# Perceiver block on one core: the order of the prelude's steps (first tokens' norm, transposes and queries ahead of the keys' weights and the first context)

## The reference, cut to what matters

```python
x = x + cross_attention(layernorm(x), ctx, ctx, mask)   # 16 heads; ctx is 32 x 257 x 256; Wq, Wk, Wv, Wo with biases
x = x + self_attention(layernorm(x))                    # rotary, causal, 16 heads
x = x + experts(layernorm(x))                           # top 2 of 8, capacity 32, hidden 1368
```

## Time and profile before

| | |
|---|---|
| median of 3 runs | 553.98 us (552.29 to 554.91) |
| span of the profiled execution, first to last instruction | 553.1 us |
| its own time outside the span | not listed; the median of the runs is 0.9 us above the span |
| PE busy | 497.3 us, 90% |
| DVE, ACT, POOL busy | 400.3, 324.7, 253.9 us |
| mean granted TensorE clock | 0.941 |

### The profile page before, as it was taken

How to read it: one execution, slowest core, us unless ns; L and a number is a source line. 1 busy time by engine, 2 the same in 40 slices (tenths; PEclk the granted TensorE clock), 3 DMA queues, 4 the chain that set the end, 5 groups by cost and what they waited for, 6 DMA issues and landing times.

```text
span 553.1 us, 18277 instructions
## 1 busy us (share of the span) xinstructions
PE 497.3 (90%) x6637; PEld 455.6 (82%) x6637; DVE 400.3 (72%) x1003; ACT 324.7 (59%) x839; POOL 253.9 (46%) x341
## 2 busy tenths in 40 slices
PE   1897999999999999999956657899999999999996
PEld 1776888888888888988845546899999999999995
DVE  2544456666767766676766797699999999999973
ACT  1455767667757775775722206756676666666650
POOL 4133344444364344536310120566767667766650
PEclk9989999999999999999996655799999999999998
DMA  6523111111111111110018000255645666457202
GB/s 181 170 78 80 42 34 29 43 40 33 33 39 39 20 39 38 39 20 3 3 9 299 1 0 1 80 163 180 191 145 170 221 191 185 127 187 227 81 1 76
DMA packets 58125, 48.91 MB, mean 88 GB/s; under 512 B 20942, under 2 KB 49744, under 8 KB 58064
## 3 DMA queue, kind: packets, MB, share of 16 engines
q1 hardware_dynamic: 58064, 48.09, 29.8%
HBM read 46.86 MB, written 1.08 MB: 87 GB/s over the span
## 4 chain that ended last, share of the span: by engine, by line
PE 79%; ACT 6%; DVE 5%; issue 5%; DMA 3%; SPq 1%; DVEq 0%; ACTq 0%; POOL 0%; POOLq 0%
PE bank L223 20%; PE bank L225 18%; PE bank L224 18%; PE bank L606 5%; PE bank L584 4%; PE bank L630 3%; PE bank L541 2%; ACT Pr L1059 2%; DMA last_prob<-Pr 2%; PE bank L989 2%; DMA w_raw<-in_L_xattn_Wk 1%; PE bank L761 1%; ACT PTd L1152 1%; PE bank L723 1%; PE bank L734 1%
## 5 line engine op out<-in xcount | busy, mean ns | idle before, releaser
L223 PE MATMUL bank<-XT_lo,W_hi 128*128 128x256 f32 (+1 forms) x352 | 100.2, 285 | 1.3 <-ACT CT L1253 1.3
L224 PE MATMUL bank<-XT_hi,W_lo 128*128 128x256 f32 (+1 forms) x352 | 99.8, 284 | 0.0
L225 PE MATMUL bank<-XT_hi,W_hi 128*128 128x256 f32 (+1 forms) x352 | 99.6, 283 | 0.0
L2000 POOL TENSOR_TENSOR W_lo<-raw,W_hi 128x256 fp32r<-128x256 f32 (+1 forms) x88 | 88.4, 1005 | 7.1
L1919 POOL TENSOR_TENSOR Pr<-Pr,rinv 128x1028 f32<-128x1028 f32 x31 | 59.0, 1903 | 47.0 <-DVE rinv L1404 46.3
L1059 ACT ACTIVATE Pr<-Sc,nmax 128x257 f32<-128x257 f32 x128 | 63.8, 502 | 23.8 <-DVE nmax L1393 19.5
L1393 DVE CUSTOM_DVE_ANT_0 Sc<-bank,mask_add 128x257 f32<-128x257 f32 x128 | 47.0, 423 | 40.8 <-PE bank L584 17.8
L1850 DVE TENSOR_TENSOR hid_lo<-hid,hid_hi 128x256 fp32r<-128x256 f32 (+1 forms) x88 | 72.5, 824 | 1.5 <-ACT hid_hi L1302 1.5
L1998 POOL CAST W_hi<-raw 128x256 fp32r<-128x256 f32 (+1 forms) x88 | 39.4, 448 | 73.4 <-PE bank L225 37.0
L1820 DVE TENSOR_TENSOR W_lo<-raw,W_hi 128x512 fp32r<-128x512 f32 (+1 forms) x88 | 69.1, 788 | 4.9 <-ACT W_hi L1226 1.3
L223 PEld LDWEIGHTS bank<-XT_lo,W_hi 128*128 128x128 f32 (+1 forms) x352 | 66.3, 188 | 1.6 <-issue 1.6
(11 more groups left out here) (237 smaller groups left out, 1345.7 us busy)
## 6 DMA issues: line engine op xcount, KB each, us to landing
raw<-in_L_ffn_w_kernel SPq DMA_DIRECT2D x32, 512.0 KB, 4.7
ctx_raw<-in_ctx SPq DMA_DIRECT2D x32, 256.0 KB, 2.8
raw<-in_L_ffn_wo_kernel SPq DMA_DIRECT2D x16, 512.0 KB, 5.8
raw<-in_L_ffn_w_kernel SPq DMA_DIRECT2D x16, 344.0 KB
last_prob<-Pr SPq DMA_DIRECT2D x128, 1.0 KB, 1.8
raw<-in_L_ffn_wo_kernel SPq DMA_DIRECT2D x8, 256.0 KB
x_sb<-in_x SPq DMA_DIRECT2D x4, 256.0 KB, 5.9
VL_all<-vl_rows SPq DMA_DIRECT2D x8, 128.0 KB
```

The source lines that it names most:

```text
L223: pe.matmul(dst, a_hi, b_lo, start=first, stop=False)
L224: pe.matmul(dst, a_lo, b_hi, start=False, stop=False)
L225: return pe.matmul(dst, a_hi, b_hi, start=False, stop=last)
L2000: po.tensor_tensor(W2_lo[0:w, m % RW, :], raw2[0:w, t, :], f(W2_hi[0:w, m % RW, :]), ALU.subtract)\
```

## The change

The list `slots` is put in another order, and the hand-written order on PE, ACT and DVE follows it. SP, POOL and every instruction's shape stay as they are; no instruction is added or removed.

```diff
-    slots = [("w", 0), ("w", 1), ("bias", 0), ("lastT", 0), ("xT", 0), ("xT", 1), ("w", 2), ("q", 0), ("q", 1), ("kl", 0), ("vl", 0)]
+    slots = [("w", 0), ("xT", 0), ("xT", 1), ("w", 1), ("bias", 0), ("q", 0), ("q", 1), ("lastT", 0), ("w", 2), ("kl", 0), ("vl", 0)]
...
-        for n in range(2):
+        for n in range(slot("w", 1) + 1):
             prepare(n)
         turn_ctx(0, 0, 16)
-        for n in range(2, slot("w", 2) + 1):
+        for n in range(slot("bias", 0), slot("q", 1) + 1):
             prepare(n)
         keys(0, 0)
-        for n in range(slot("q", 0), slot("vl", 0)):
+        for n in range(slot("lastT", 0), slot("vl", 0)):
             prepare(n)
...
-        for n in range(2):
+        for n in range(slot("w", 1) + 1):
             prepare(n)
         split_ctx(0, 0)
-        for n in range(2, slot("w", 2) + 1):
+        prepare(slot("bias", 0))
+        ac.wait_ge(sm["first_act"], slot("bias", 0) + 1)
+        for n in range(slot("q", 0), slot("q", 1) + 1):
             prepare(n)
-        ac.wait_ge(sm["first_act"], slot("bias", 0) + 1)
         keep_keys(0, 0)
-        for n in range(slot("q", 0), slot("vl", 0)):
+        for n in range(slot("lastT", 0), slot("vl", 0)):
             prepare(n)
...
         low(slot("w", 0))
+        norm_tokens(0)
+        low(slot("xT", 0))
+        low(slot("xT", 1))
         low(slot("w", 1))
-        norm_tokens(0)
         split_ctx(0, 0)
         low(slot("lastT", 0))
-        low(slot("xT", 0))
-        low(slot("xT", 1))
         low(slot("w", 2))
```

## The result

The changed kernel takes 555.4 us (median of 20 runs, 552.99 to 559.52) against 552.72 us before (20 runs on the same chips, 551.29 to 557.99). The ratio is 1.0046, 95% interval 1.0025 to 1.0067: slower, by an amount near the 0.5% of the prediction's bound. The predicted 553.3 us pointed the other way, and 555.4 lies just outside the range.

What follows compares the result with a forecast made beforehand. The prediction took the run to hang on when ACT keeps `vl`, just before 28.03 us. Terms summed to +0.2 or -1.4 us by the clock's rise; -0.7 from 553.98 gave 553.3 us, range 551.3 to 555.3.

Steps and rivals of the forecast that it cites:

- the prediction's bound: Whole kernel: a change of 0.5%, 2.8 us, counts as faster or slower; staying within it was given 0.88.
- One cost the rows do not show: First four norm tiles on DVE beside POOL's two clearings: bounded by nothing and 3.0 us, taken as 0.1 us.
- The prediction's own sign of being wrong: In the changed profile's prelude: the prediction is wrong if DVE's norm waits for POOL; no size given.
- rival 3: First norm held by POOL's clearings until 14.28: +1.7, 555.7 us, or +3.3, 557.3 with a later clock; chance 0.08.
- the forecast's -1.4: Prelude up to `vl`: the sum of the change in us if PE's clock rises before the queries.
- rival 1: Before `kl`: the wait for Wv's parts eats the gain, -0.2 to +0.2 us, 554.0 us; chance 0.25.
- (b): PE's queries and keys: clock rises three microseconds earlier than 18.9, before the queries; `kl` starts at 22.35, 1.5 us stay.
- the middle of +0.2 and -1.4: Sum for the prelude, between clock rising at 18.9 again and rising before the queries: taken as -0.7 us.
- one to one to the end: From ACT keeping `vl`, just before 28.03, to the program's end: any shift of this event passes on in full.
- The base of 553.98: Whole kernel: the time of the kernel before, in us, from which -0.7 gave the forecast 553.3.
- What the Trainium skill says of transposes: PE's prelude: full clock does not engage for transposes, so only queries from 15.65 on would wake it.

Runs made afterwards that it cites:

- after_again_2: The changed kernel, unchanged, in a third profiled execution: 555.79 us, ratio 1.0007 to the kernel before.
- after_again: The changed kernel, unchanged, in a second profiled execution: 555.09 us, ratio 1.0022 to the kernel before.
- after: The changed kernel in its first profiled execution, against the kernel before: span 553.2 us, time 555.01 us.
- after_clear_early: The changed kernel with POOL's clearings of PTd and Vm moved ahead of its wait for the first variance: 552.40 us, ratio 0.9958 to the kernel before.

## Why the prediction was wrong

**The step that failed** is "One cost the rows do not show". I bounded the norm beside the clearings by 0 and 3.0 us and took 0.1, "because the later rows show a norm slowed and not held". The first tile measured 3.17 us in place of 0.40, 2.77 us more: the upper bound, nearly to the tenth. The prediction's own sign of being wrong, DVE's norm waiting for POOL, came with it.

Rows 8 were misread, for they show the hold. POOL's timeline of the kernel before, beside the norm at 82.65:

```profile
82.58 0.40 POOL L1892 TENSOR_TENSOR Qb<-QT,tab 128x128 f32<-128x128 f32 x1
82.93 0.25 POOL L1895 COPY KT<-KLT 128x2 f32<-128x2 f32 x1
```

POOL's instruction began 0.07 us before the tile and ended at 82.98; the tile ended at 83.13, 0.15 later. Under the clearings it ended 0.14 to 0.15 after POOL as well, with one, two and three of them. So the tile at 82.65 was held to the end of its neighbour too; 0.33 us were left of the neighbour, and with the 0.15 that makes the 0.48, only 0.07 more than the 0.41 of a tile alone. The same pair stands six times in this profile, with tiles of 0.48, and the copy on POOL behind it takes 0.25 beside the tile where it takes 0.19 elsewhere, as if POOL waited in its turn. A cost that lasts as long as the neighbour's instruction cannot be read from the duration beside a short neighbour; it has to be read from where the tile ends. The rule of the Trainium skill (SBUF — State Buffer, section Who interferes with whom), to which rival 3 gave 0.08, was borne out by the very rows that were held against it. Why DVE gets its turn between these two POOL instructions and not between two clearings stays open.

**Rival 3** is what happened. It had xT0 at 15.12 (15.24 measured), `kl` at 25.6 (25.84) and 555.7 us (555.4). The shift of `vl` is not its +1.7 but 3.1 us in the profiled run, 3.0 in `after_again_2` and 0.6 in `after_again`, with the clock falling at other moments. That its 555.7 met the 555.4 is partly luck: it adds 1.7 to a base of 553.98, while the medians are 2.7 apart from a base of 552.72.

**The rest of the sum.** With the hold taken away the forecast can be checked. xT0 was to start at 12.06: 12.16. The wait from the keys' end to `kl` with an idle of 1.9: 1.52. `kl` between 22.35 and 24.0: 23.11. There the forecast's -1.4 breaks down all the same, in a second step that failed: I took everything from `kl` on as before, 4.1 us. `kl` starts 0.8 earlier than before, but the clock falls half a microsecond into it, and from its start to `vl` going out it takes 4.92 us, so `vl` goes out at 28.03. So even without the hold `vl` would have been where rival 1 had it, unmoved, though about half by rival 1's wait and half by the clock. With Wv moved the wait vanished, and the clock stayed up until long after `vl`. Two slips of the sum are small: (b) starts its queries at 15.5 where the text had 15.65, and the middle of +0.2 and -1.4 is -0.6, not -0.7.

**What held.** All hangs on when `vl` is kept. In eleven profiled executions the time from `vl` going out to the exponentials of sequence 2 is 18.7 to 19.0 us where it lands in 1.5 us, and 20.4 to 20.9 where it lands in 3.0 to 3.1, whatever the order before it: 28.07 to 46.76 and 31.15 to 49.94, for instance. So the shift passes on one to one as far as these exponentials. Beyond them it does not hold to the tenth: from there to the end of the span all fourteen profiles together take 498.7 to 506.1 us, a spread larger than the change, so the forecast's "one to one to the end" is not shown by single profiles. The chain through SP's queue alone, as I read it from rows 2 and 3, is also not the whole: where the landing is early SP waits for POOL's normalising before last_prob (issued at 42.91, right behind it), and the first energies that this comes from stand on PE behind `vl`. In the two executions of the kernel before the small DMAs go out at 39.85 and 39.83 alike, and land 2.1 us apart, behind loads that began 1.5 us apart.

**The base of the sum.** The base of 553.98 was the median of three runs, 1.3 us above the 552.72 of twenty, and the rows came from a profiled execution with a late landing, which goes with 2.1 us (48.88 against 46.76), while the kernel after was profiled with an early one. That is most of the reason why two equal spans stand beside medians 2.7 us apart; the rest lies in the spread after the exponentials.

**The clock.** What the Trainium skill says of transposes (TensorE: Matmul & The Clock Gate, section Part 4: PE-mode transpose), weighed in the prediction, was not borne out. With the clearings early PE did 3.8 us of transposes from 12.16 on, and the queries, from 15.96, had the full pace after two matmuls: 0.23 us between starts from 16.9 on. That is close to case (b) of the sum. The second execution of the kernel after is plainer still. PE's rows of `after` and then of `after_again`, the transposes of context 0:

```profile
17.85 1.06 PE L541 MATMUL bank<-tab,ctx_raw 128*128 128x128 f32 x4
```

```profile
17.48 0.76 PE L541 MATMUL bank<-tab,ctx_raw 128*128 128x128 f32 x4
18.17 0.22 PE L469 MATMUL bank<-tab,bias_raw 6*128 6x6 f32 x1
18.34 0.47 PE L223 MATMUL bank<-xnT_lo,WT_hi 128*128 128x512 f32 x1
```

The same four take 0.76 us in place of 1.06, and the first product comes only at 18.34: the clock rose while PE had done nothing but transposes since 14.87.

## What to carry to other kernels

Before an instruction of VectorE is moved to an earlier place, look at what GpSimd does there. A VectorE instruction of the norm's form (one fp32 tensor and two scalars, on SBUF) waits out whole clearings, and the clearings here had no near deadline, so they belong where both engines are idle; or give the VectorE instruction its two-input form. Putting the work of the longer chain at the head of an in-order queue makes everything behind it wait for that chain; the order before let PE do Wk and context 0 in the meantime. And take a second profile of the kernel before, where a change of half a per cent matters: one late landing in it went with 2.1 us, nearly as much as the change. And judge whether one engine is held by another from where the two end, not from a duration alone.

## What the runs showed of the hardware

A DMA of 32 KB landed in 1.5 us or in 3.0 to 3.5 us, the late ones with a transfer of instructions (16 KB) among its packets; the same kernel shows both. The norm tile, a one-input VectorE instruction on SBUF, does not get done beside a clearing on POOL: 0.40 us becomes 1.43, 3.18 and 4.92 beside 1.4, 3.1 and 4.9 us of clearings, and in each of these the tile ends 0.14 to 0.15 after POOL, also behind a POOL instruction of 0.40 us. The two-input form runs at 0.48 us inside a clearing. The granted clock fell to 0.50 in the middle of the prelude behind two microseconds with PE busy for 0.48 (`after`) and within such a stretch of 0.89 (`after_clear_early`); in `after_again`, with 0.91 and then 1.75, it stayed at 1.00 until 28 us, and with Wv moved beyond 36 us. It rose once during transposes alone (`after_again`).
